# A twelve-head decayed attention laid out as eight heads and four, with its states, its carried products and its output projection cut into row and column tiles of the array

## What is computed

```python
q = silu(x @ Wq).reshape(b, n, h, d).transpose(0, 2, 1, 3)
k = silu(x @ Wk).reshape(b, n, h, d).transpose(0, 2, 1, 3)
v = silu(x @ Wv).reshape(b, n, h, d).transpose(0, 2, 1, 3)
diff = idx[:, None] - idx[None, :]
decay = jnp.where(diff >= 0, jnp.exp(log_slope[:, None, None] * jnp.maximum(diff, 0.0)), 0.0)
energy = jnp.einsum('bhnd,bhmd->bhnm', q, k) * decay
out = jnp.einsum('bhnm,bhmd->bhnd', energy, v)
out = out.transpose(0, 2, 1, 3).reshape(b, n, e)
out = out * jax.nn.sigmoid(x @ Wg1 @ Wg2)
out = _layernorm(out @ Wo, ln_w, ln_b)
```

## Time and profile before

| | us |
|---|---|
| median of 3 runs (1266.52 to 1268.34) | 1266.62 |
| the profiled execution's own time | 1269.04 |
| its span, first to last instruction | 1267.3 |
| phase 1, about | 12 to 986 |
| phase 2, about | 986 to 1168 |
| phase 3, about | 1168 to 1267 |

### The profile page before, as it was taken

The page is one execution under the profiler, slowest core; times in us unless marked ns, Lnnn a source line. Parts: engine busy times, 40 slices in busy tenths (PEclk is TensorE's granted clock), DMA queues, the critical chain, the costliest instruction groups (busy, mean ns, idle before and its releaser), DMA issues.

```text
span 1267.3 us, 34978 instructions
## 1 busy us (share of the span) xinstructions
PE 1180.8 (93%) x12938; PEld 958.6 (76%) x12938; DVE 815.9 (64%) x2114; ACT 735.8 (58%) x1677; POOL 571.8 (45%) x878
## 2 busy tenths in 40 slices
PE   5999999999999999999999999999999999997653
PEld 4888888888888888888888888888887555554432
DVE  4577777767777777777676777777776122222897
ACT  5456666767766767766677677676763211111566
POOL 3355554555555555555454555454543100000664
PEclk8999999999999999999999999999999999999555
DMA  4411121111111111112111111111135699997786
GB/s 144 189 49 52 56 79 55 54 56 55 51 51 51 51 51 51 51 53 71 66 54 51 60 51 51 51 51 51 51 126 212 246 421 423 422 424 258 214 261 186
DMA packets 50653, 158.34 MB, mean 125 GB/s; under 512 B 5354, under 2 KB 31328, under 8 KB 38308
## 3 DMA queue, kind: packets, MB, share of 16 engines
q1 hardware_dynamic: 33016, 145.04, 31.0%
q10 hardware_dynamic: 17600, 12.78, 3.2%
HBM read 132.18 MB, written 25.62 MB: 125 GB/s over the span
## 4 chain that ended last, share of the span: by engine, by line
PE 78%; DVE 16%; issue 2%; ACT 1%; SPq 1%; DVEq 1%; DMA 1%; POOL 0%; ACTq 0%; POOLq 0%
PE ps L945 11%; PE ps L946 10%; PE ps L947 10%; DVE p_sb L801 7%; PE ps L1005 7%; PE ps L1040 6%; PE ps L1219 5%; PE ps L1238 4%; PE ps L1083 3%; PE ps L988 3%; PE ps L989 3%; PE ps L1023 2%; DVE res L914 2%; PE ps L1252 2%; PE ps L1243 2%; DVE st L920 2%
## 5 line engine op out<-in xcount | busy, mean ns | idle before, releaser
L423 POOL TENSOR_TENSOR xl<-x_sb,xh 128x392 fp32r<-128x392 f32 x192 | 189.2, 1019 | 86.2 <-DVE gn L776 78.0
L801 DVE TENSOR_TENSOR p_sb<-ps,dec 98x1176 f32<-98x1176 f32 x128 | 176.9, 1382 | 56.3 <-PE ps L1005 56.3
L1005 PE MATMUL ps<-qm,kT 32*98 32x196 f32 x1536 | 117.0, 343 | 9.6 <-DVE p_sb L801 7.5
L1040 PE MATMUL ps<-p_sb,vpad 98*32 98x98 f32 x3072 | 112.9, 251 | 1.9 <-DVE p_sb L801 1.9
L656 ACT ACTIVATE hg<-ps 128x768 f32<-128x768 f32 x32 | 26.0, 811 | 147.6 <-PE ps L1243 147.6
L1040 PEld LDWEIGHTS ps<-p_sb,vpad 98*32 98x32 f32 x3072 | 84.8, 110 | 35.4 <-issue 24.7
L1005 PEld LDWEIGHTS ps<-qm,kT 32*98 32x98 f32 x1536 | 75.2, 158 | 35.1 <-DVE p_sb L801 23.0
L906 DVE COPY y2st<-ps 128x192 f32<-128x192 f32 x32 | 11.5, 358 | 120.4 <-PE ps L1219 120.4
L740 DVE BATCH_NORM_STATS2 st<-ps 98x6 f32<-98x192 f32 x128 | 40.0, 355 | 71.1 <-PE ps L947 71.1
L467 POOL TENSOR_TENSOR invn<-nrm,expo 98x4 f32<-98x4 f32 x32 | 32.7, 1021 | 117.7 <-DVE nrm L786 117.4
L673 ACT ACTIVATE o_sb<-res,nb,rstd 98x192 f32<-98x192 f32 x128 | 59.6, 536 | 43.2 <-DVE nb L929 42.5
(11 more groups left out here) (186 smaller groups left out, 3631.0 us busy)
## 6 DMA issues: line engine op xcount, KB each, us to landing
x_sb<-in_xT SPq DMA_DIRECT2D x32, 1176.0 KB, 5.1
w1v<-in_fc SPq DMA_DIRECT2D x32, 1152.0 KB, 10.6
w2v<-in_fc SPq DMA_DIRECT2D x32, 1152.0 KB, 13.1
h_dram<-h SPq DMA_DIRECT2D x32, 294.0 KB
h2r<-h_dram SPq DMA_DIRECT2D x32, 294.0 KB
out<-o_sb ACTq DMA_DIRECT2D x32, 294.0 KB
comb_dram<-cst SPq DMA_DIRECT2D x32, 98.0 KB, 1.7
cbuf<-comb_dram SPq DMA_DIRECT2D x32, 98.0 KB, 3.9
```

The costliest lines, as they stand in the source:

```text
L423: pool.tensor_tensor(xl[:, k], x_sb[:, k], xh[:, k].bitcast(F32), ALU.subtract)\
L801: dve.tensor_tensor(dst, src, rate.unsqueeze(2).to_broadcast([T, PAIRS, 2, TOK]), ALU.mult)\
L1005: mm = pe.matmul(ps[0:T, SC_AT + r, mt * TOK:(mt + 1) * TOK].rearrange("p (b n) -> p b n", b=2), kT[rows, g, n], qm[rows, g, :, n], start= ...
L1040: mm = pe.matmul(ps[32 * b:32 * b + 32, 5 + g, a * TOK + mt * T:a * TOK + mt * T + T], vpad[:, 2 * a + mt, 32 * (g * HG + h):32 * (g * HG ...
```

## The change

The heads become eight and four. The first eight fill 128 rows (`kA`, `qA`, images side by side, 392 columns); the last four are 64 rows, and the two images are put on top of each other (`kB`, `qB`, 128 rows by 196 columns). There are now three rounds of scores, decay and values in a step instead of four, each with four row or column groups instead of three. States are twelve 32-column products that give only the 32 x 32 blocks, carried products use 32 x 32 tiles of the array, and `project_out` makes the eight heads' part with 128 rows and the four heads' part with two 64-row halves that alternate, one for each image. Token tiles are therefore taken as (x, 2+x), each in a bank of its own. Projections are 128 and 64 (queries: 80) columns wide instead of 96 and 96 (112). The queries of the second chunk are no longer a third activation on ACT: POOL adds the two masked halves and then scales. The second half of V's rows, the logits and `cosines` move to later places. The decay table has 16 columns of heads instead of 12.

```diff
-            def project_out(j, x):
+            def project_out(j, x, d_before):
                 pe.wait_ge(ogl_rdy, 2 * j + 2)
-                for t in (2 * x, 2 * x + 1):
-                    for k in range(2):
-                        n = slice(t * T, (t + 1) * T)
-                        mm = product(ps[0:T, 2 + x, (t % 2) * D:(t % 2) * D + D],
-                                     ogh[:, k, n], ogl[:, k, n], woh[:, k], wol[:, k], k == 0, k == 1)
...
+                for a in range(2):
+                    n = slice((2 * a + x) * T, (2 * a + x + 1) * T)
+                    product(ps[0:T, SC_AT + 2 * x + a, 0:D], ogh[:, n], ogl[:, n], woh[:, 0], wol[:, 0], True, False)
+                n = slice(PT + x * T, PT + (x + 1) * T)
+                for o, w in ((ogh, wol), (ogl, woh), (ogh, woh)):
+                    for a in range(2):
+                        rows = slice(DB * a, DB * a + DB)
+                        mm = pe.matmul(ps[0:T, SC_AT + 2 * x + a, 0:D], o[rows, n], w[rows, 1],
+                                       start=False, stop=(o is ogh and w is woh))
                 mm.then_inc(wo_mm, 1)
...
             def scores(i, k, c):
...
-                    n = slice(a * TOK + mt * T, a * TOK + mt * T + T)
-                    for r in range(PAIRS):
+                    n = slice(k * TOK + mt * T, k * TOK + mt * T + T) if k < 2 else slice(mt * T, mt * T + T)
+                    for r in range(4):
                         rows = slice(32 * r, 32 * r + 32)
+                        keys, queries = (kA, qA) if k < 2 else (kB, qB)
                         mm = pe.matmul(ps[0:T, SC_AT + r, mt * TOK:(mt + 1) * TOK].rearrange("p (b n) -> p b n", b=2),
-                                       kT[rows, g, n], qm[rows, g, :, n], start=True, stop=True)
+                                       keys[rows, n], queries[rows, :, n], start=True, stop=True)
...
             def states(i):
...
-                for g, a in ORDER:
-                    v = vpad[:, 2 * a].rearrange("p (j q d) -> p j q d", q=4, d=HD)
-                    mm = pe.matmul(ps[0:G, 6, (2 * g + a) * G:(2 * g + a + 1) * G]
-                                   .rearrange("p (j q d) -> p j q d", q=2, d=HD),
-                                   kts[:, a, g * G:(g + 1) * G], v[:, 3 * g:3 * g + 3, 0:4:3, :],
-                                   start=True, stop=True)
+                for x in range(3):
+                    for r in range(4):
+                        a, pair = (x, r) if x < 2 else (r // 2, HA // 2 + r % 2)
+                        v = vpad[:, 2 * a].rearrange("p (j q d) -> p j q d", q=4, d=HD)
+                        mm = pe.matmul(ps[32 * r:32 * r + 32, 7, 2 * HD * x:2 * HD * x + 2 * HD]
+                                       .rearrange("p (q d) -> p q d", q=2),
+                                       kts[:, x * DA + 32 * r:x * DA + 32 * r + 32], v[:, pair, 0:4:3, :],
+                                       start=True, stop=True)
...
-            def carried(i, k):
...
+            def carried(i, g):
+                for x in ((0, 1), (2,))[g]:
+                    for r in range(4):
+                        rows, at = slice(32 * r, 32 * r + 32), (x * TOK if x < 2 else 0) + T
+                        mm = pe.matmul(ps[rows, 6 + g, at:at + T], state[rows, x], qd[rows, x],
+                                       start=False, stop=(x > 0))
...
-                    for g in range(2):
-                        act.wait_ge(q_mm, 2 * i + g + 1)
-                        act.activation(qm[:, g, 0], ps[0:G, g, 0:PT], ACT.Silu, scale=parity[:, 0:1])
-                        act.activation(qm[:, g, 1], ps[0:G, g, 0:PT], ACT.Silu, scale=parity[:, 1:2])
...
+                    act.activation(qA[:, 0], ps[:, 0, 0:PT], ACT.Silu, scale=parity[:, 0:1])
+                    act.activation(qA[:, 1], ps[:, 0, 0:PT], ACT.Silu, scale=parity[:, 1:2]).then_inc(q_sb, 1)
...
+                    for a in range(2):
+                        for b in range(2):
+                            last = act.activation(qB[DB * a:DB * a + DB, b], ps[0:DB, 1, a * TOK:(a + 1) * TOK],
+                                                  ACT.Silu, scale=parity[0:DB, b:b + 1])
...
 # PE's step, the part behind the projections of the queries
+                    rows_of_v(i, 0)
...
+                    pe.wait_ge(q_sb, 2 * i + 1)
+                    project(i, 0, wkh, wkl, k_mm)
+                    if d:
+                        pe.wait_ge(hb_sb, i + 1)
+                        logits(i - 2)
+                    pe.wait_ge(q_sb, 2 * i + 2)
+                    pe.wait_ge(zl_rdy, i + 1)
+                    project(i, 1, wkh, wkl, k_mm)
                     scores(i, 0, c)
+                    gate(i)
...
+                    rows_of_v(i, 1)
                     keys_turned(i)
```

More of the change, by code:

```diff
@@ L33 @@
 HD = D // H
-HG = H // 2
+HA = 8
+HB = H - HA
+DA, DB = HA * HD, HB * HD
+COLS = PT + TOK
+HX = HA + 2 * HB
 RANK = 16
@@ L543, in _ @@
             act.wait_ge(dist_st, 4)
-            for h in range(H):
-                act.activation(dec[:, h, :], dist[:, :], ACT.Exp, scale=slope[:, h:h + 1]).then_inc(dec_exp, 1)
+            for h in range(HX):
+                c = h if h < HA else HA + h
+                act.activation(dec[:, h, :], dist[:, :], ACT.Exp, scale=slope[:, c:c + 1]).then_inc(dec_exp, 1)
             act.activation(kdec[:, :], slope[:, :], ACT.Exp, scale=left[:, 0:1]).then_inc(tables, 1)
@@ L563, in step @@
                 if c:
-                    for g in range(2):
+                    for g, n in enumerate((slice(0, PT), slice(PT, COLS))):
                         act.wait_ge(og_sb, 2 * i - 1 + g)
-                        act.activation(ogh[:, g], og[:, g], ACT.Copy).then_inc(ogh_rdy, 1)
+                        act.activation(ogh[:, n], og[:, n], ACT.Copy).then_inc(ogh_rdy, 1)
                 if d:
@@ L587, in step @@
-                    for row in (0, ZT):
[L588 to L593, removed]
@@ L594, in step @@
[L594 to L596 removed]
+                    act.wait_ge(q_mm, 2 * i + 1)
+                    act.activation(qA[:, 0], ps[:, 0, 0:PT], ACT.Silu, scale=parity[:, 0:1])
+                    act.activation(qA[:, 1], ps[:, 0, 0:PT], ACT.Silu, scale=parity[:, 1:2]).then_inc(q_sb, 1)
+                    act.wait_ge(q_mm, 2 * i + 2)
@@ new lines, in step @@
+                    act.wait_ge(k_mm, 2 * i + 1)
+                    act.activation(kA[:, :], ps[:, 0, 0:PT], ACT.Silu).then_inc(k_sb, 1)
+                    act.wait_ge(k_mm, 2 * i + 2)
+                    for a in range(2):
+                        last = act.activation(kB[DB * a:DB * a + DB], ps[0:DB, 1, a * TOK:(a + 1) * TOK], ACT.Silu)
+                    last.then_inc(k_sb, 1)
+                    if c:
+                        act.wait_ge(og_sb, 2 * i)
+                    act.wait_ge(g_mm, 2 * i + 1)
@@ L597, in step @@
+                    act.activation(gt[:, 0:PT], ps[:, 0, 0:PT], ACT.Tanh, scale=0.5).then_inc(g_sb, 1)
+                    act.wait_ge(g_mm, 2 * i + 2)
+                    for a in range(2):
+                        last = act.activation(gt[DB * a:DB * a + DB, PT:COLS], ps[0:DB, 1, a * TOK:(a + 1) * TOK],
+                                              ACT.Tanh, scale=0.5)
+                    last.then_inc(g_sb, 1)
+                    turned_v(i, 1)
                 if c:
@@ L603, in step @@
                         act.activation(squares[0:T, t], gn[0:T, t], ACT.Square, accum_out=ss[:, t:t + 1]).then_inc(ss_rdy, 1)
[L604 to L608, removed]
-                        act.activation(gt[:, g], ps[0:G, g, 0:PT], ACT.Tanh, scale=0.5).then_inc(g_sb, 1)
                 if d:
@@ L744, in first_norm @@
                 dve.drain()
-                for t in (2 * x, 2 * x + 1):
+                for t in tiles(x):
                     dve.bn_aggr(mv1[:, t, :], st1[:, t, :]).then_inc(mv1_rdy, 1)
@@ L1138, in step @@
                     h_turned(i, 0)
-                if d:
-                    if not a and not c:
-                        idle_products(0, 6)
+                if d and not a:
+                    if not c:
+                        idle_products(1, 6)
                     logits(i - 2)
@@ L1181, in step @@
                     scores(i, 2, c)
+                    if not d:
+                        carried_ready(i)
                     values(i, 1)
@@ L1184, in step @@
                     if a:
-                        pe.wait_ge(g_sb, 2 * i + 2)
+                        carried_ready(i)
                     else:
-                        idle_products(0, 16 if c else 4)
+                        idle_products(1, 16 if c else 4)
                     dispatch_turned(i - 2)
                     if not a:
-                        idle_products(0, 2)
+                        idle_products(1, 2)
                 if a:
                     carried(i, 0)
-                    carried(i, 1)
-                    scores(i, 3, c)
-                    values(i, 2)
                 if d:
```

(9 more changed lines are left out.)

297 lines of the change are left out of this document (156 added, 141 removed).

## The result

| | us |
|---|---|
| before, median of 4 runs | 1266.67 (1266.52 to 1268.34) |
| changed kernel, median of 4 runs | 1220.41 (1219.3 to 1221.7) |
| ratio | 0.9633, 95% interval 0.9620 to 0.9646 |
| profiled execution, span | 1219.0 |

A forecast was written before the change was run, and what follows sets the result against it. PE's list plus a few waits for DVE was taken to bound the step. The terms summed to -1.26, said as -1.3 us a step, about -41 us in all, giving 1225 us with a range of 1214 to 1241.

The forecast's parts named there:

- output projection: PE's `project_out`: halves abreast save 0.26 us, shape changes and load cost 0.33, for each x; +0.14 us a step.
- keys: Second half of the keys: 64-column shape costs 0.1 + 0.05 us, the 0.26 us wait goes; -0.11 us a step.
- first to second scores: PE between these scores: 0.18 us wait covered by V's moved rows, gate's 64-wide product costs shape and loads; +0.13 us a step.
- second to third scores: Third scores wait for the second decay, 2.82 us in all against 2.50 now; +0.32 us, PE waiting 0.6 to 1.1.
- third scores to next step: One round of scores and values and part of the carried work go: 6.92 us becomes 5.18; -1.74 us a step.
- change of shape: On PE, a product of another tile shape than its neighbour costs 0.1 us; seven such changes added in a step.
- Slack ahead of the second scores: Second scores: DVE's decay ready after 4.67 us, PE there after 4.85, from the keys' second half; slack 0.2 us.
- The rival in which DVE becomes the beat: Cosines and tokens 0.5 us later than reckoned lose 0.3 us a step at the second scores; 1235 to 1245 us, chance 0.15.
- The start: ACT makes 16 decay columns instead of 12, 1.1 us more, hidden by PE's 2.2 us wait for DVE's slots.
- floor at 28 ns: Rival: matmuls start no closer than 28 ns, so four abreast costs +0.6 us a step; 1245 us, chance 0.13.
- serial fourth tile: Rival: the fourth tile does not run beside the other three, +4.0 us a step, net +2.7; 1310 us, chance 0.03.
- Cheaper shapes: Rival: shape changes cost under 0.1 us or the states' wait is shorter; at nothing -2.0 us a step, 1203 us; chance 0.07.

The follow-up runs named there:

- The filler runs: Changed kernel with 14 or 4 idle 128 x 128 products put ahead of the third scores: 1294.57 us with 14, 1224.65 us with 4.
- gap-filling kernels: Changed kernel with the logits' transposes moved behind the states and DVE's and ACT's work reordered: 1210.96 us; with DVE's list mended and ACT's old order: 1202.81 us.
- The run with the early rounding: Changed kernel with ACT rounding the first images behind 10 of the 16 decay exponentials instead of behind all and the tables: 1219.41 us.
- run with three tiles: Changed kernel without the fourth row or column tile of scores, values, states and carried products: 1219.74 us.

## Why the prediction held, and where it was off

The mechanism and the sign were right; the step fell by 1.50 us where I summed 1.26 and rounded to 1.3. By my own terms, in us a step, read from the rows above:

| stretch | predicted | measured | from |
|---|---|---|---|
| output projection | +0.14 | 0.00 | 521.26 to 522.33 is 1.07, as before |
| keys | -0.11 | -0.28 | 502.73 to 503.83 and 505.19 to 506.37: 2.28 against 2.56 |
| first to second scores | +0.13 | -0.03 | 3.45 less the moved half of V, 1.07: 2.38 against 2.41 |
| second to third scores | +0.32 | +0.34 | 2.84 against 2.50 |
| third scores to next step | -1.74 | -1.65 | 5.27 against 6.92 |

The measured rows sum to -1.62. The other 0.12 lies in blocks that I had put at nothing: among them the transposes behind the 64-row halves (0.66 us for `gn`, 522.33 to 522.99, where they took 0.62, and 0.48 for `hT` where they took 0.44). So part of the closeness is luck: terms that were too dear by 0.47 us together stand against 0.23 us a step that was too cheap or missing, and about 1 us at the start.

**The term that was mis-sized is the change of shape**, in its 64-column cases. I had read 0.1 us for each from the earlier trace rows and applied it to products that go from 128 to 64 columns with full rows. These start 0.17 to 0.21 us apart, and widening them gives nothing back. The price in the earlier trace rows is real: values to states pays it with the same 98 rows and 96 columns instead of 32 (0.81 against 0.70 us), so it is not a matter of rows alone. Why 128 to 64 columns goes free is not shown. That is 0.15 us in the keys and most of the 0.31 us (shapes and loads) in the gate. From 128 to 64 rows the price is there too: into the halves 521.71 to 521.89 is 0.18, where 0.09 is usual. The output projection's part from 521.71 to 522.33 is 0.62 us, 0.26 more than four slots of 0.09, and three slots were saved, so changes and loads eat just what the halves gain. It gives nothing, as I had said, and costs nothing either.

**Second to third scores** came as summed: the decay of 1568 elements lasts 1.79 us and PE waits 0.91. The filler runs show that the wait is real slack of 0.97 us.

**Slack ahead of the second scores.** I gave 0.2 us: 4.67 for DVE and 4.85 for PE from the start of the second half of the keys. It is 4.63 (505.19 to 509.82), DVE's figure, since PE does not pay my shape prices. The rival in which DVE becomes the beat is thus half true: the slack is gone, but DVE was not late by more than I reckoned, and nothing was lost against the sum. This chain is where the gap-filling kernels gained.

**The moved logits.** I counted only the 0.26 us wait of the old place. Undoing the move costs 1.12. The term was right for the sum, since with the logits moved there is no wait at all. But the text gave no sign that moving half of V's rows away opens a wait of 1.1 us at the keys, which only the logits cover.

**The start.** I said that 1.1 us of more exponentials hide behind PE's wait for DVE's slots. They did not: that wait stayed (2.27 us), and the first product of the queries stood at 25.52 instead of 24.39, because DVE's work ahead of the slots was itself later: `wvl` lasted 1.84 us beside POOL's later and longer work on `dec`, where it had taken 0.56. The run with the early rounding shows the way back. It cost about 1 us.

**The other steps.** I gave about 1 us each to steps 0, 1 and 31. Phase 1 as a whole ends 48.3 us sooner (938.22 against 986.55); 29 steps of 1.50 are 43.6, and the start took 1 us back, so about 6 us lie in the three steps without full flags and the tail. Step 1 lasts 25.45 us where it was 27.37 (by the starts of its first product). Phases 2 and 3 take 280.8 us as before.

**Rivals.** No floor at 28 ns and no serial fourth tile (run with three tiles). Cheaper shapes came true for the 64-column products alone, which is why the time fell 5 us below the forecast and not 22. The page of the Trainium skill named in the prediction gives a floor of 25 ns, which the values' 22 ns pass under.

## What to carry to other kernels

Count how many tiles of the array a layout leaves empty: with the fourth row and column group filled, each block did a third more work for about 0.01 us. Then look at what the new list uncovers, here two waits on other engines of 1 us each. The wait at the keys opened because work was moved away, and the logits cover it (32 us); into the other went the transposes of the logits, with a better order on DVE (17.6 us). When an instruction of DVE is moved, see what POOL runs at its new place.

## What the runs showed of the hardware

- Products on different row groups of the array do not wait for each other's place in the program: three of one half followed by three of the other took 0.46 us, and 0.44 when they alternate.
- A change from 128 to 64 columns with full rows costs nothing that these runs can tell in float32r; a change from 128 to 64 rows costs 0.09 us and the weight load (0.08 us); a change from 32 to 96 columns with 98 rows costs 0.11 us in float32 (values of 0.81 against 0.70).
- DVE's `Lc`, an operation with both inputs in SBUF, took 416 ns with POOL idle, 814 beside POOL's splits and 1129 in another place beside them; `cmx` and `kts` there stayed at 0.42 and 0.55. The Trainium skill, page "SBUF — State Buffer", section "Who interferes with whom", says that a DVE instruction with two SBUF inputs contends with a POOL instruction that reads SBUF. The traces agree. The page says that casts can contend too: `gw` at the start agrees (1.08 against 0.24 us), while the cast of `wvh` at 18.14 took 0.35 us beside POOL's `dec`, as it did with POOL idle.
- A float32 product of 128 x 128 by 128 that is repeated takes two records of 0.11 us, 0.22 us in all. That is the scores' pace: a record of 196 columns takes 0.166 us there, which makes 0.108 for 128.
